# Two edge attentions: each use of TensorE's results stands about one turn later in the order

## What is computed

```
score[e,h] = sum_d q'[dst[e],h,d] * key[src[e],h,d]     # layer 0: keys and values by relation (8 types)
                                                        # layer 3: key + 0.2 * rel[relation[e]] (64 types)
m[node,h]  = max over the node's edges of score
ex[e,h]    = exp(score[e,h] - m[dst[e],h])
out[node]  = sum over edges of ex * value[src[e]] / sum over edges of ex
```

## Time and profile before

| | |
|---|---|
| median of 3 runs | 6596.09 us |
| the profiled execution | 6543.18 us |
| its span | 6541.5 us |
| PE, weight loads | 4303.1 us (66%), 3112.8 us (48%) |
| DVE | 3451.9 us (53%) |
| ACT | 2183.4 us (33%) |
| POOL | 3085.2 us (47%) |
| DMA | 1064.02 MB, mean 163 GB/s |

### The profile page before, as it was taken

The page is one execution under the profiler, slowest core; times in us unless marked ns, Lnnn a source line. Parts: engine busy times, 40 slices in busy tenths (PEclk is TensorE's granted clock), DMA queues, the critical chain, the costliest instruction groups (busy, mean ns, idle before and its releaser), DMA issues. The chain is left out here.

```text
span 6541.5 us, 93657 instructions
## 1 busy us (share of the span) xinstructions
PE 4303.1 (66%) x24913; PEld 3112.8 (48%) x24913; DVE 3451.9 (53%) x6696; ACT 2183.4 (33%) x7656; POOL 3085.2 (47%) x3083
## 2 busy tenths in 40 slices
PE   5996677777777662555555628886656666666666
PEld 3664455445454431333333527774335555555553
DVE  4553666666666663222222221113568888888885
ACT  1222455545554521000000102222235545545551
POOL 0432556666666326667766230003156656656651
PEclk8997777777777886666777869997878888888885
DMA  4334666666666516333333138752456666666653
GB/s 136 128 127 149 191 200 198 199 204 200 198 196 195 166 53 198 91 94 93 93 89 93 34 109 269 261 194 85 159 177 204 208 207 209 203 201 206 208 176 106
DMA packets 530773, 1064.02 MB, mean 163 GB/s; under 512 B 118922, under 2 KB 346540, under 8 KB 526817
## 3 DMA queue, kind: packets, MB, share of 16 engines
q0 software_dynamic: 199152, 603.78, 31.5%
q1 hardware_dynamic: 322670, 452.44, 20.8%
q10 hardware_dynamic: 8512, 2.74, 0.2%
HBM read 951.27 MB, written 194.54 MB: 175 GB/s over the span
## 5 line engine op out<-in xcount | busy, mean ns | idle before, releaser
L793 POOL DMA_INDIRECT l3e_kv<-t_table,k_recs x912 | 973.3, 1067 | 663.4 <-ACT l3e_vw L1070 368.8
L793 POOL DMA_INDIRECT l0e_kv<-t_table,k_recs x912 | 973.3, 1067 | 635.1 <-ACT l0e_vw L1070 373.2
L1500 PE MATMUL l2e_pA<-l2e_row,l2e_oh 128*128 x1824 | 590.1, 486 | 673.9 <-issue 388.5
L1447 POOL DMA_INDIRECT l2e_row<-t_table,l2e_srcw x808 | 801.7, 992 | 353.7 <-issue 242.9
L1500 PEld LDWEIGHTS l2e_pA<-l2e_row,l2e_oh 128*128 128x128 f32 x1824 | 425.8, 243 | 838.2 <-issue 766.3
L1027 PE MATMUL l0e_pA<-l0e_vw,l0e_ohf 128*128 128x260 f32 x1824 | 659.0, 500 | 187.3 <-issue 124.4
L979 PE MATMUL l3e_pQE<-l3e_qb,l3e_ohT 128*128 128x256 bf16 x2736 | 426.2, 317 | 398.7 <-issue 370.7
L1070 ACT ACTIVATE l0e_vw<-l0e_kv,l0e_w 128x64 f32<-128x64 f32 x2736 | 679.9, 334 | 0.0
L1070 ACT ACTIVATE l3e_vw<-l3e_kv,l3e_w 128x64 f32<-128x64 f32 x2736 | 679.7, 334 | 0.0
L1471 DVE SCALAR_TENSOR_TENSOR l2e_acc<-l2e_acc,k_itf,l2e_pA 128x257 f32<-128x257 f32 x228 | 109.5, 480 | 924.5 <-issue 859.3
L1027 PEld LDWEIGHTS l0e_pA<-l0e_vw,l0e_ohf 128*128 128x128 f32 x1824 | 421.7, 244 | 349.5 <-issue 196.1
(11 more groups left out here) (476 smaller groups left out, 7099.9 us busy)
## 6 DMA issues: line engine op xcount, KB each, us to landing
exp_w<-in_L_gnn_w SPq DMA_DIRECT2D x224, 512.0 KB
t_table<-l0n_tab SPq DMA_DIRECT2D x26, 2048.0 KB, 6.8
l0e_qb<-t_q SPq DMA_DIRECT2D x228, 192.0 KB
l3e_qb<-t_q SPq DMA_DIRECT2D x228, 192.0 KB
t_agg<-l0e_acc SPq DMA_DIRECT2D x228, 130.0 KB
t_agg<-l3e_acc SPq DMA_DIRECT2D x228, 130.0 KB
l0e_drow<-t_drow SPq DMA_DIRECT2D x57, 512.0 KB
l3e_drow<-t_drow SPq DMA_DIRECT2D x57, 512.0 KB
```

Of the source, the lines that this page charges most:

```text
L793: pool.indirect_dma_start(kv[:, n % SK, g, :], None, table[:, :], bass.IndirectOffsetOnAxis(ap=K["recs"][:, n, g, ridx:ridx + 1], axis=0)) ...
L1447: pool.indirect_dma_start(row[:, w % SR, g, 0:D], None, table[:, :], bass.IndirectOffsetOnAxis(ap=srcw[:, w, g:g + 1], axis=0)).then_inc(r ...
L1500: last = pe.matmul(pA[i % PB][:, 0:W], oh[:, s, g, :], row[:, bass.ds(held, 1), g, :].rearrange("p o c -> p (o c)"), start=(g == 0), stop= ...
```

## The change

The work is the same: the same instructions with the same shapes. Three things differ.

1. The order of the turns. `weigh`, `widen` and ACT's `weigh` are those of item t - 3 instead of t - 1, `sums` that of t - 4 instead of t - 2, `rescale` and `merge` those of t - 5 instead of t - 3. The chain of a block stands in four turns: `run_max` and `run_ends` late in j = 0, `turn_ends` and `spread` in j = 1, `candidates` to `drop_new` and `shift` in j = 2, `shifted` and `weights` in j = 3.
2. The rooms. Row slots SK are 12 in l0e and 11 in l3e (10 before), q slots QL are 7 in l0e (8 before; l3e stays at 4), `ohT` has 3 buffers (2), `drow` one (2), `prod` one (2). The scratch of l0e's start (`dT`, `etb`, `dlf`) lies in the memory of `vw`, which is first written later.
3. SP's order. `load_queries(n)` stands ahead of `load_rows`, `load_rows(n // 4 + 1)` is issued at n % 4 = 2 instead of 0, and the stores stand 14 items behind instead of 12.

```diff
-        SK = 10
+        SK = 12 if first else 11
-        QL = 2 * QS if first else QS
+        QL = 7 if first else QS
+        TS = 3
+        LATE = 14
-        ohT = S.sb("ohT", [P, 2, BI * G, P], BF16)
-        drow = S.sb("drow", [P, 2, BI * G * P], BF16)
+        ohT = S.sb("ohT", [P, TS, BI * G, P], BF16)
+        drow = S.sb("drow", [P, BI * G * P], BF16)
-        prod = S.sb("prod", [P, 2, G, D])
+        prod = S.sb("prod", [P, G, D])
...
-                if m >= 2:
-                    sp.wait_ge(ohT_ready, m - 1)
+                if m >= 1:
+                    sp.wait_ge(ohT_ready, m)
...
-            for n in range(1, NI + 12):
+            for n in range(1, NI + LATE):
                 if n < NI:
-                    if n % BI == 0 and n // BI + 1 < NBT:
+                    load_queries(n)
+                    if n % BI == 2 and n >= BI and n // BI + 1 < NBT:
                         load_rows(n // BI + 1)
-                    load_queries(n)
...
+                if n:
+                    dve.wait_ge(sc_ready, n)
...
-                n, r, x = t + BI, t - 3, t - 1
+                n, r, x = t + BI, t - 5, t - 3
...
-                if 0 <= t - 2 < NI:
-                    sums(t - 2)
+                if 0 <= t - 4 < NI:
+                    sums(t - 4)
+                if live(m) and j == 2:
+                    shift(m)
```

More of the change, by code:

```diff
@@ L820, in turned_onehots @@
             def turned_onehots(m):
[L821 to L825, removed]
+                dve.wait_ge(drow_in, 16 * (m + 1))
+                if m >= TS:
+                    dve.wait_ge(qe_ps, BI * (m - TS + 1))
+                    dve.wait_ge(sh_ps, m - TS + 1)
+                dve.tensor_scalar(ohT[:, m % TS, :, :].rearrange("p k e -> p (k e)"), drow[:, :], K["pidx"][:, 0:1], None, ALU.is_equal).then_inc(ohT_ready, 1)
                 if not first:
                     dve.wait_ge(erow_in, 16 * (m + 1))
+                    if m >= 2:
+                        dve.wait_ge(qe_ps, BI * (m - 1))
                     dve.tensor_scalar(ohrT[:, m % 2, :, :].rearrange("p k e -> p (k e)"), erow[:, :], K["pidx"][0:R64, 0:1], None, ALU.is_equal).then_inc(ohrT_ready, 1)
@@ L933, in _ @@
                     products(n)
+                if live(m) and j == 2:
+                    candidates(m)
+                if live(m) and j == 3:
+                    shifted(m)
+                if 0 <= r < NI:
+                    merge(r)
+                if live(m) and j == 2:
+                    block_max(m)
+                if n < NI:
+                    scores(n)
                 if live(m) and j == 0:
                     run_max(m)
[L936 to L946, removed]
+                if live(m) and j == 2:
+                    node_max(m)
                 if j == 2 and m + 2 < NBT:
                     turned_onehots(m + 2)
+                if live(m) and j == 2:
+                    drop(m)
                 if j == 3 and m + 1 < NBT:
@@ L952, in _ @@
                     weigh(x)
+                if live(m) and j == 0:
+                    run_ends(m)
+                if live(m) and j == 2:
+                    drop_new(m)
         @block.tensor
@@ L978, in queries @@
                     for i in range(3):
-                        last = pe.matmul(pQE[n % 2][:, g, :], ohT[:, m % 2, G * j + g, :], qb[:, n % QL, i, :], start=(i == 0), stop=(i == 2))
+                        last = pe.matmul(pQE[n % 2][:, g, :], ohT[:, m % TS, G * j + g, :], qb[:, n % QL, i, :], start=(i == 0), stop=(i == 2))
                 if not first:
@@ L1016, in shift @@
                 for c in range(BI * G):
-                    last = pe.matmul(pSh[:, c, :], ohT[:, m % 2, c, :], mxb[:, m % 2, :, 1 + c // G], start=True, stop=True)
+                    last = pe.matmul(pSh[:, c, :], ohT[:, m % TS, c, :], mxb[:, m % 2, :, 1 + c // G], start=True, stop=True)
                 last.then_inc(sh_ps, 1)
```

49 lines of the change are left out of this document (22 added, 27 removed).

## The result

The changed kernel takes 6798.78 us (median of 4 runs, 6790.34 to 6809.1), the kernel before 6598.33 us beside it (4 runs, 6587.59 to 6609.09). The ratio is 1.0298, with a 95% interval of [1.0281, 1.0315]. Predicted were 6137 us and 5990 to 6400. The experiments came to several chips, and on one of another kind the same pair gives 0.9794 [0.9774, 0.9814] (e9). Why both hold is what the experiments are about.

What follows compares the result with a forecast made beforehand. DVE's waits for PE's results, chained to ACT and POOL, were taken to bound both attentions. Gains of 281 us (l0e) and 200 (l3e) less 22 for the ends gave 459, so 6137 us, range 5990 to 6400.

Steps and rivals of the forecast that it cites:

- the first reading: Both attentions: a better order can give the distance from blocks of 28.0 and 28.5 us to the engines' floors.
- wrong altogether: Sign that the forecast fails as a whole: a block of over 27 us in both attentions.
- Step 1: Spread to candidates: with the transposes, spread and candidates set in separate turns, the 3.19 us of lateness go.
- Step 2: Shift to z: about 3 us of work stand between; DVE still stands 4.5 us a block, or nothing.
- Step 3: Merge, in l0e 4.72 us late: sums and merge stay one turn apart; bounds 0 and 1.4 us.
- Step 4: z to weigh: about 4 us instead of 1.2 before DVE's use; ACT's wait of 417.9 us shrinks by itself.
- Step 5: SP queue: q loads no longer held up behind the erow wait; PE's 6.92 us gap goes.
- Step 6: Row slots held two turns longer: lead suffices, cost nothing; POOL rarely blocked, its waits of 230.2 and 217.9 us go.
- Step 7: Shared scratch (prod with one slot, dlf, dT, etb in vw): products wait for one-turn-old scores; cost nothing.
- five signs of being right: POOL's vw wait under 80 us, over 152 and 163 items, SP wait within 10 us, L979 gaps within 4 us, clock over 0.85.
- The first: Rival: running gathers keep PE's results late, so only small steps gain: 6483 us, half effect 6290 to 6400; chance 0.20.
- The second: Rival: spread idle time puts PE at 1.2 GHz in every turn, making it the bound: around 6780 us; chance 0.10.

Runs made afterwards that it cites:

- e9: The changed kernel itself, with no further edit, on a fast chip: 5806.59 us against 5927.22 us for the kernel before, ratio 0.9794.
- e13: The changed kernel with each gather of both attentions from item SK on replaced by a GpSimd memset, on a slow chip: 5793.08 us.
- e12: The changed kernel with each gather of both attentions from item SK on replaced by a GpSimd memset, on a fast chip: 5619.18 us.
- e10: The kernel before itself, with no edit, profiled on a fast chip, where it takes 5927.22 us.
- e4: The kernel before with only the change's SP order (q rows ahead of row loads, those two items later), on a slow chip: 6657.78 us, ratio 1.0165.
- e11: The changed kernel with 10 row slots in both attentions, on a fast chip: ratio 0.9816 to the kernel before.
- e14: The changed kernel with 10 row slots in both attentions, on a slow chip: ratio 1.0309 to the kernel before.
- e3: The changed kernel with POOL's second, third and fourth gathers of an item each waiting for a DVE step, on a slow chip: 6503.33 us, ratio 0.9934.

## Why the prediction was wrong

**The step that failed is the first reading**: "the distance between 28 and these floors is what a better order can give". On a chip with prompt results the same kernel before, with the same order, needs 21.8 us a block in l0e and 25.9 in l3e. So of l0e's distance of 6.6 us to POOL's floor, 6.2 hung on the chip: the lateness of PE's results and what follows from it. The prediction put all of it down to the order; the new order removed none of it on such a chip (28.8 us a block in l0e and 31.9 in l3e, what the prediction had named as "wrong altogether"), and with pacing 1.5 us of l0e's. That the 6.2 is lateness and no other slowness of the chip rests on e13: without gathers the slow chip has blocks of 18.6 us, the fast one (e12) 18.8.

The rows had it. The earlier trace rows has L1017 end at 1408.2 and its reader at 1415.66, and I wrote down "7.5 us on". What I did not ask is what went on in those 7.5 us: the gathers ran until 1413.53, and the semaphore event of the result stands at 1415.64, 2.1 us after the last. The row of the kernel before that shows it:

```profile
1412.58 0.95 POOL L793 DMA_INDIRECT l0e_kv<-t_table,k_recs  x1 [0.30 <-issue]
```

I laid part of it to PE at 1.2 GHz. As a small part the runs do not rule this out (e13 was granted 0.92 and 0.90, not 0.75 and 0.81), but in e9 and e13 the events come 0.01 us after the end, so there is no such lateness there.

**Steps 1, 2, 3** (candidates, z, merge). On the slow chip: candidates 100.1 to 64.4 us in 1000, z 104.2 to under 10, merge 146.4 to 108.8. Step 2 did what it should, under 0.3 us a block in place of the 4.5 feared. Step 1 did a third of it: its 3.19 us were to go, and 64.4 us in 1000 are 1.9 us a block. Step 3 stayed over its bound, 3.1 us a block against 1.4. The larger part of the miss is that the late results met a fourth reader, the products L847 (193.5 us in l0e) and the keys L840 (234.9 in l3e), for which the sum has no term. "What is late next" in my text was POOL's gathers; it was the query products.

**Step 4** (z to weigh): ACT's 417.9 us at fac went, and 467.1 us at L1071 (362.1 and 105.0, for the sums' a_ps) came.

**Step 5** (SP): right in its mechanism. PE's gap goes (e10, e9). On the slow chip it turned against the kernel: alone it costs 1.65% there (e4). That the gap had stopped DVE, hence POOL, and so given POOL a second rest in the block is my reading of e4; only the rests and the cost are measured.

**Step 6** (slots): "rarely blocked" holds on the fast chip (9.7 + 0.6 us in 1000, l0e) and fails on the slow one (254 us in l0e, 305 in l3e). Slots were priced at nothing below the lead, and e11 and e14 agree. **Step 7** at nothing: no run speaks against it.

**The sum.** The blocks forecast for the changed kernel, 22.8 and 24.8 us, are what it has on a fast chip within 1 us (22.2 and 23.8). But there the kernel before stands at 21.8 and 25.9, so 57 x 2.1 = 120 us are gained in l3e and 57 x 0.4 = 23 lost in l0e, 97 of the 98.4 us between the spans (5905.2 and 5806.8), a fifth of the 459. All five signs of being right hold for the changed kernel on that chip (672 and 722 gathers in 1000 us, POOL's wait for slots 71 us or less, no SP wait over 0.4 us at the erow load, no gap before L988 of l3e over 4 us, clock 0.88 and 0.91). They describe the kernel after alone, so they could not tell that the kernel before would stand there too.

**The rivals.** The first named the cause ("if running gathers delay PE, a schedule that never blocks POOL has that always") and got the sign of the change wrong: it let the three small steps keep their gain (6483 us) and had no price for late results at other readers. What it gave as its mark, waits for merge and z of over 200 us with the clock near 1.0, did not appear: they were 118.6 us in l0e, at a clock of 0.80. The waits of over 200 us for PE lay at L840, and nearly 200 at L847. Its argument against itself, that l3e's chain ran beside gathers and cost little, was sound for the kernel before (mean lateness 0.83 us) and not for the changed one (1.91). The second came close in time (6780), and DVE did wait for query products as it said, but by luck, for another reason: the clock was 0.81 and higher than before in l0e (0.75), and DVE's new wait ended on a late event, not on a slow product (0.52 us for L995 x12). The Trainium skill ("SBUF — State Buffer", "Who interferes with whom") says that "PE and ACT never wait on anyone". It speaks of ports to SBUF; it does not speak of the whole path from PE's product to its reader. There the slow chips show waits of up to 10.8 us on DVE (L847) and 11.8 on ACT (L1071) beside gathers, and 0.01 us from PE's end to the event without them.

What stays open: whether it is PE's writes to PSUM or only its semaphore events that come late, or whether the last products run later than their modelled records say; what differs between the chips; what decides how late a result is; how short a rest would do; and what pacing costs the changed kernel on a fast chip. No version was measured that wins on both: e3's is the best on slow chips, the changed kernel on fast ones.

## What to carry to other kernels

Before crediting a wait to the order, compare the end of the producer's record with the start of its reader, and where they are more than a few tenths apart look at what every other engine did in between. A change that only takes waits away can cost time (e4: 1.65%), because another engine's bursts and rests move with it, so price those as well. And where a kernel leans on gathers from GpSimd, measure on more than one chip before trusting a sign: here the same pair gave 1.03 and 0.98.

## What the runs showed of the hardware

- In the sets of runs with the kernel before at 6548 to 6598 us, PE's results reached their readers up to 10 us and more late while GpSimd issued indirect DMAs at a stretch. Of the results that were over 3 us late, most came 1.5 to 2.5 us after the last gather of a stream (74 of 125 in l0e before, 24 of 40 in l3e of the changed kernel); the others came within a stream. On the chips with 5917 to 5927 us the mean was 0.01 to 0.06 us, also where GpSimd never rested. 64-byte rows in place of 2 KB changed nothing; memsets in place of gathers took it away in the attentions, while l2e, which kept its gathers, had 3.4 us on the mean in the same run.
- The stage l2e, whose gathers no kernel here changes, takes 1155 us from its first to its last gather in e13 and 1038 in e12, so such a chip costs it some 116 us more.
- POOL issues a gather each 1.36 to 1.39 us on the mean when it is not blocked (1000 / 734, 1000 / 722, or 22.2 / 16), single ones 1.25 us apart, and with a drain before each one in 4.2 us.
